# A gate applied to two projections apart, with the sum moved to GpSimd

## The reference

```
attn = windowed_attn(xn, W_qkv, W_O, b_O)      # 16 heads, windows of 64
ug = xn @ W_ug + b_ug
g = sigmoid(ug[..., S_DIM:])
states: s = A * s + (xn @ B_w + u)             # a scan over the tokens
y_ssm = states @ C_w
x = x + g * attn + (1.0 - g) * y_ssm
```

## Time and profile before

| what | value |
|---|---|
| median of 3 runs | 1922.1 us (1920.32 to 1922.23) |
| profiled execution, first to last instruction | 1963.7 us |
| mean granted TensorE clock | 0.973 of full speed |
| mixer stage | from 0 to about 818 us |
| one batch of the mixer | about 48 us |

### The profile page before, as it was taken

One profiled execution on the slowest core, in us unless ns is written; L12 is line 12 of the kernel. 1 busy time (PEld: TensorE's weight loads), 2 busy tenths in 40 slices (PEclk: granted clock), 3 DMA queues, 4 the chain that ended last, 5 costly groups with the idle time before them and its releaser, 6 DMA issues. The chain is left out here.

```text
span 1963.7 us, 66143 instructions
## 1 busy us (share of the span) xinstructions
PE 1768.1 (90%) x23600; PEld 1357.0 (69%) x23601; DVE 1414.5 (72%) x3235; ACT 1000.3 (51%) x1810; POOL 1074.9 (55%) x1304
## 2 busy tenths in 40 slices
PE   4999999999999999799888988809999999999997
PEld 2677776777777677466555655508888888888886
DVE  7788888888888887478778878744656656656665
ACT  3444444444444444455464555306665565565564
POOL 5333334444333332457777777754666666666664
PEclk8999999999999999899999999959999999999998
DMA  5322222222222222254344345313545545555553
GB/s 153 90 77 79 73 72 72 72 72 73 72 73 74 73 75 69 93 162 140 112 139 147 112 129 155 95 34 81 93 89 94 88 92 94 89 91 94 90 91 56
DMA packets 165756, 183.06 MB, mean 93 GB/s; under 512 B 37188, under 2 KB 146439, under 8 KB 165440
## 3 DMA queue, kind: packets, MB, share of 16 engines
q1 hardware_dynamic: 111360, 105.03, 19.2%
q0 software_dynamic: 36352, 56.78, 15.7%
q10 hardware_dynamic: 17856, 18.37, 2.7%
HBM read 109.14 MB, written 62.38 MB: 87 GB/s over the span
## 5 line engine op out<-in xcount | busy, mean ns | idle before, releaser
L1980 POOL DMA_INDIRECT out<-experts_y,experts_entry x144 | 237.2, 1647 | 192.6 <-DVE experts_y L1956 162.6
L1921 DVE TENSOR_SCALAR experts_v<-experts_v 128x512 f32<-128x512 f32 x144 | 73.8, 512 | 227.6 <-ACT experts_v L1895 213.7
L856 ACT ACTIVATE mixer_prob<-mixer_sc 128x1024 f32<-128x1024 f32 x128 | 131.2, 1025 | 165.9 <-PE mixer_sc L699 165.9
L1895 ACT ACTIVATE experts_g<-experts_pg,x_b 128x256 f32<-128x256 f32 x288 | 120.7, 470 | 184.1 <-PE experts_pv L132 184.0
L1970 POOL DMA_INDIRECT experts_rows<-scratch_xs,experts_entry x144 | 169.2, 1175 | 50.6 <-issue 50.3
L987 DVE TENSOR_REDUCE w_mx<-mixer_sc 128x8 bf16<-128x1024 f32 x128 | 156.3, 1221 | 22.7 <-PE mixer_sc L673 22.7
L130 PE MATMUL experts_pg<-experts_xT,x_w 128*128 128x256 f16 x576 | 158.2, 275 | 11.8 <-issue 8.0
L1603 POOL DMA_INDIRECT scratch_queue<-mlp_entry,mlp_slot x128 | 139.1, 1087 | 43.9 <-issue 39.3
L130 PE MATMUL experts_py<-x_w,experts_hh 128*128 x576 | 157.7, 274 | 2.0 <-DVE experts_hl L1933 2.0
L1116 POOL TENSOR_TENSOR mixer_oTl<-mixer_on,mixer_oTh 128x128 f16<-128x128 f32 x128 | 54.8, 433 | 190.4 <-ACT mixer_oTh L866 190.1
L132 PE MATMUL experts_py<-x_w,experts_hl 128*128 x576 | 157.8, 274 | 0.0
(11 more groups left out here) (378 smaller groups left out, 5699.0 us busy)
## 6 DMA issues: line engine op xcount, KB each, us to landing
w_Kz<-mixer_Kt SPq DMA_DIRECT2D x64, 128.0 KB, 2.7
mixer_hres<-mixer_h SPq DMA_DIRECT2D x16, 512.0 KB, 4.4
scratch_xs<-scratch_mod SPq DMA_DIRECT2D x64, 128.0 KB, 3.5
scratch_x<-w_x SPq DMA_DIRECT2D x16, 512.0 KB, 2.9
scratch_n<-w_x SPq DMA_DIRECT2D x32, 256.0 KB, 2.3
w_nrm<-scratch_n SPq DMA_DIRECT2D x16, 512.0 KB, 4.3
mlp_stage<-in_x_w SPq DMA_DIRECT2D x16, 512.0 KB, 4.1
mlp_xb<-scratch_x SPq DMA_DIRECT2D x16, 512.0 KB
```

The costliest lines, as they stand in the source:

```text
L856: act.activation(prob[:, n % 2, :].rearrange("p (c j) -> p c j", c=2), sc[:, 2:4, :], ACT.Exp, scale=SCALE).then_inc(exped.sem, 1)
L1895: act.activation(dst[:, q, f * ROWS:(f + 1) * ROWS], bank[:, q, f * ROWS:(f + 1) * ROWS], fn, bias=x["b1"][:, bass.ds(e, 1), bias + 2 * q ...
L1921: dve.tensor_scalar(v[:, q, :], v[:, q, :], -8.0, 10.0, ALU.max, ALU.min).then_inc(v_cut.sem, 1)
L1980: pool.indirect_dma_start(out=out, out_offset=bass.IndirectOffsetOnAxis(ap=entry[:, s, t, 0:1].bitcast(I32), axis=0), in_=y[:, s % 2, t, : ...
```

## The change

The state output is no longer subtracted on TensorE. The left half of the PSUM bank now holds attention alone, and `nc` and its three matmuls for each tile are gone. GpSimd turns tanh into the gate g = 0.5 tanh + 0.5, in two operations of 128x512 for each batch. VectorE makes share = attention x g and mix = (g - 1) x state output. GpSimd sums share + hres, and then subtracts mix: two operations for each tile where there was one.

```
-    def negate(self, dve):
-        dve.wait_ge(self.low.sem, 6)
-        for part in range(2):
-            dve.tensor_scalar(self.w["nc"][part][:], self.w["c"][part][:], -1.0, None, ALU.mult
-                              ).then_inc(self.shaped.sem, 1)
...
+        share = m.sb("share", [P, TT, D])
...
# TensorE, outputs(b, t)
-                hi_lo_products(pe, att, [sth[:, tok], stl[:, tok]], [a[:, 0, :] for a in w["nc"]], False, False)
...
# VectorE, mix_tokens(b, t)
                 if t == 0:
-                    dve.wait_ge(gate_sb.sem, gate_sb.at(b, 2))
+                    dve.wait_ge(opened.sem, opened.at(b, 2))
+                    dve.wait_ge(x1_part.sem, x1_part.at(b, 0))
                 dve.wait_ge(out_mm.sem, out_mm.at(b, t + 1))
-                dve.scalar_tensor_tensor(out=mix[:, t, :], in0=mix[:, t, :], scalar=1.0, in1=out_bank[t][:, 0:D],
-                                         op0=ALU.add, op1=ALU.mult).then_inc(gated.sem, 1)
+                dve.tensor_tensor(share[:, t, :], out_bank[t][:, 0:D], mix[:, t, :], ALU.mult).then_inc(gated.sem, 1)
                 dve.wait_ge(gated.sem, gated.at(b, t + 1))
-                dve.scalar_tensor_tensor(out=mix[:, t, :], in0=mix[:, t, :], scalar=0.5,
-                                         in1=out_bank[t][:, D:], op0=ALU.mult, op1=ALU.add
-                                         ).then_inc(mixed.sem, 1)
+                dve.scalar_tensor_tensor(out=mix[:, t, :], in0=mix[:, t, :], scalar=-1.0, in1=out_bank[t][:, D:],
+                                         op0=ALU.add, op1=ALU.mult).then_inc(mixed.sem, 1)
...
# GpSimd, body(b, last)
                 inverse_deviation(NB if last else b + 1, 1)
+                for u in range(2):
+                    wait_alone(pool, gate_sb.sem, gate_sb.at(b, u + 1), pool_passed)
+                    pool.tensor_scalar(mix[:, 2 * u:2 * u + 2, :], mix[:, 2 * u:2 * u + 2, :], 0.5, 0.5, ALU.mult,
+                                       ALU.add).then_inc(opened.sem, 1)
                 if last:
                     for j in range(6, 9):
                         start.low_part(pool, j, start.low)
...
                 for t in range(TT):
+                    pool.wait_ge(gated.sem, gated.at(b, t + 1))
+                    pool.tensor_tensor(x1[:, t, :], share[:, t, :], hres[:, t, :], ALU.add).then_inc(x1_part.sem, 1)
+                    pool.wait_ge(x1_part.sem, x1_part.at(b, t + 1))
                     pool.wait_ge(mixed.sem, mixed.at(b, t + 1))
-                    pool.tensor_tensor(x1[:, t, :], mix[:, t, :], hres[:, t, :], ALU.add).then_inc(x1_sb.sem, 1)
+                    pool.tensor_tensor(x1[:, t, :], x1[:, t, :], mix[:, t, :], ALU.subtract).then_inc(x1_sb.sem, 1)
```

More of the change, by code:

```diff
@@ L497, in mixer @@
         gate_sb = m.counter("gate_sb", 2)
+        opened = m.counter("opened", 2)
         gated = m.counter("gated", TT)
+        x1_part = m.counter("x1_part", TT)
         mixed = m.counter("mixed", TT)
@@ L776, in body @@
                     if s == NW:
-                        made_once(b, (start.shaped, 3))
+                        made_once(b, (start.shaped, 1))
                         outputs(b, 0)
@@ L980, in body @@
                         start.low_part(dve, j, start.low)
-                    start.negate(dve)
                 if not last:
@@ L2043, in program @@
                 halves("c", 1, D)
-                halves("nc", 1, D)
                 for name in ("bg3", "bo3"):
```

## The result

| | median | lowest to highest | runs |
|---|---|---|---|
| before | 1921.49 us | 1920.32 to 1922.23 | 4 |
| changed | 1934.3 us | 1931.66 to 1936.43 | 4 |

The ratio is 1.0069, with an interval of 1.0057 to 1.0081: the change costs 13.3 us by the ratio. The direction was as forecast and the time lies in the range; the loss is 2.2 times the +5.9 of the point.

A forecast was written before the change was run, and what follows sets the result against it. TensorE was taken to bound the mixer, with GpSimd time before the first oTl reaching it undiminished. The terms -16.5 + 20.7 + 1.7 = +5.9 us gave 1928.0 us, range 1920 to 1944.

The forecast's parts named there:

- Part 1: TensorE's outputs at the batch seam: dropping 192 products with nc returns 1.10 us a seam, -16.5 us.
- Part 2: GpSimd before the first oTl: two gate openings, 1.31 us a pair, reach TensorE undiminished, +20.7 us.
- Rivals one and three: Gate openings: one, the pair costs 2.3 us, 1944, chance 0.10; three, the pair costs nothing, 1907, chance 0.08.
- rival four: Near balance: the pair costs 1.2 us and the seam returns the full 1.31; +1.0, 1923 us, chance 0.20.
- Part 3: GpSimd's eight x1 sums delay SyncE's store, keys and hres copy; TensorE's 0.56 us idle covers the keys; priced at nothing.
- Rival two: Late modulate on GpSimd collides with VectorE's scan, costing 1.0 us in 14 batches; 1942 us, chance 0.20.
- Part 4: Mixer's end, behind the last batch: no seam hides the eight x1 sums, +1.7 us.

The follow-up runs named there:

- e2: Changed kernel with SyncE's store of x1 issued in the next batch, behind the keys and the copy to hres; 1922.74 us, ratio 1.0000.
- e5: Kernel before without the three products with nc and nothing in their place, so the state output is not subtracted; 1899.83 us, ratio 0.9894.
- e4: Kernel before with only the pair of gate openings added, writing a tile nobody reads, mix_tokens waiting for it; 1941.1 us, ratio 1.0087.
- e8: Changed kernel with the store of x1 moved behind the next batch's keys but ahead of the copy to hres; 1926.68 us, ratio 1.0018.
- e6: Kernel before with each x1 sum made twice, first into a tile nobody reads; 1926.28 us, ratio 1.0032.
- before again: Kernel before, unchanged, run and profiled a second time; 1919.6 us, ratio 0.9999, profiled span 1917.6 us.
- e1: Changed kernel with the two gate openings ahead of the second inverse deviation on GpSimd; 1918.78 us, ratio 0.9973.
- e9: Changed kernel with x1's store behind keys and hres copy, and openings plus last batch's low parts ahead of the second inverse deviation; 1901.72 us, 0.9886.
- e7: Changed kernel with the store of x1 issued by GpSimd right behind its sums, and SyncE's store gone; 1928.33 us, ratio 1.0030.

## Why the prediction was partly right

**Part 1, the products: right.** `outputs(0)` was to give 0.33 and gave 0.34 (C). The rest of the seam was to give 0.77: in e2 and e5, where the keys are on time, D fell by 0.80 and 0.84. In the changed kernel this was earned and taken back at the next step.

**Part 2, the pair: right, a little high.** An opening took 623 ns for my 0.67, and two take 1.21 for 1.31; an estimate from the earlier trace rows of an operation that the trace did not have was 7% off. The estimate by the Trainium skill, GPSIMD Engine Reference, sections 3.1 and 4.1, was 0.64, and the 623 ns agree with it. A grew by 1.20, so the wait passed through VectorE, the copy to `shift` and TensorE undiminished, as the last batch had shown. e4 gives the term alone as +16.7 instead of +20.7; 2.7 of the 4.0 are the 0.19 a batch in B, of which below. Rivals one and three are out. Of rival four, the pair's 1.2 us came true and the seam's full 1.31 did not (1.14).

**Part 3, the sums: this is the step that failed.** The text had the sums taking 6.57 us from the start of the first one, and they took 6.44 (326.46 to 332.90). It had the keys start 7.42 behind that point, and they started 7.51 behind. It had the last key land 12.6 behind (339.9 against 327.28), and TensorE went on 13.75 behind. I took the last key's flight as 2.7 us, the median of all 64 transfers of before; it took 4.1 (336.06 to 340.16). The four transfers now follow the 512 KB store by 0.9 us (333.07 to 333.97), where before it was 2.1. I had TensorE want the keys at 339.57 and covered the rest with 0.56, leaving 0.23 us to spare by a sum of five terms, and wrote "Price nothing". The true figure is 0.84 to 0.89 us a batch, 12.6 in 15. The text did give the price for the case that the cover is gone, a us for a us, but it gave that case no chance, and none of the rivals was it.

The margin was smaller than the spread that the trace of before showed: the keys' landing there has its median at 2.7 us and its maximum at 4.4. It is also a wrong reading of the batch shown. There the last key did not land near 338.9 but at 340.37, 4.1 us behind its issue, and the fourth transfer of a batch took 3.4 to 4.4 us in 8 of 15 batches of before (3.9 or more in 14 of 15 after the change). With 4.1 in place of 2.7 the prediction's own sum has the key land at 341.3 against 340.13, so 1.2 us a batch instead of nothing. The late flight was there before the change; the change took away the time that hid it.

That the time lies in the range owes something to luck. The upper part of the range stood there for rivals one and two, and neither of them is what filled it.

**Rival two: real, smaller, and hidden here.** `modulate` did start late and ahead of the scan (341.40 against 342.58), and the scan's median rose from 1993 to 2183 ns, its maximum to 2467, not over 3000. The keys had delayed the scan itself, and the two met less than in e8, where `modulate` starts some 0.7 us ahead of the scan and not 1.2: A of the changed kernel (18.71) is that of e2 (18.73), where the scan takes 1998. So it cost nothing in the changed kernel, and 0.28 a batch where it was provoked in e8.

**Part 4, the end: right in kind, a little small.** The extra sums were to cost 1.7, and with the last batch's 1.3 for the pair the stretch from the last scan to the MLP was to grow by 3.0. It grew by 3.4, and a further 0.9 followed. Alone, the parts give +2.9 (sums, e6), -0.9 (products, e5) and +2.0 (pair, e4) in this stretch. The rows, of the changed kernel and then of before again:

```profile
804.94 0.61 PE L684 MATMUL mixer_sc<-w_twoI,w_maskq 64*128 64x512 bf16 x2 [9.59 <-DVE w_shift L1005]
...
824.41 0.72 POOL L1123 TENSOR_TENSOR w_x<-w_x,mixer_mix 128x256 f32<-128x256 f32 x1
...
826.33 1.94 PE L1290 MATMUL mlp_pj<-w_identf,w_nrm 128*128 128x128 f32 x8 [5.80 <-PEq L405]
```

```profile
812.14 0.72 POOL L1122 TENSOR_TENSOR w_x<-mixer_mix,mixer_hres 128x256 f32<-128x256 f32 x1 [0.70 <-DVE mixer_mix L957]
...
814.05 1.10 PE L1289 MATMUL mlp_pj<-w_identf,w_nrm 128*128 128x128 f32 x8 [2.91 <-PEq L411]
```

TensorE now idles 5.80 us instead of 2.91 ahead of the MLP, and its first eight transposes then take 1.94 us instead of 1.10. That this is the 0.9 is not shown: in e4 and e5 the idle time is 2.91 and the transposes take 1.06, and yet the time from there to the end is 1105.3 and 1106.0 us, against 1103.6 in before again and 1104.4 in the changed kernel.

**What was not foreseen and went the other way.** B lost 0.19 us a batch. TensorE had paused without a releaser ("issue") for a moment before L721 in the profiles of before:

```profile
321.58 0.42 PE L721 MATMUL mixer_pv<-mixer_prob,w_halfone 128*32 128x128 f32 x5 [0.16 <-issue]
```

The two profiles of before differ in B as well (9.77 and 9.51), and B is 9.32 also in e4, which keeps the products. So it is not the products, and the cause stays open; with a kernel that differs from itself by 0.26, it may not be an effect of the change at all. It is worth 2.7 us of the account.

**The sum.** In the pieces of the account, forecast and measured against before again:

| piece | forecast | measured |
|---|---|---|
| up to the second scan: a seam and batch 0's pair | -1.10 + 1.10 = 0 | -1.05 |
| 14 periods | 14 x (1.31 - 1.10) = +2.9 | +9.9 |
| last scan to the MLP: the last pair and part 4 | 1.3 + 1.7 = +3.0 | +3.4 |
| behind it | 0 | +0.9 |
| sum | +5.9 | +13.2 |

The 7.0 us too few in the periods are the keys, +11.8 (0.84 x 14), less three things that went better than forecast: B, -2.7; the pair, -1.5 (0.11 x 14); the products, -0.6 (1.14 for 1.10). The first piece was not taken apart, and its -1.05 is within what two profiles of before differ by. Without the keys' 11.8 the change would stand at +1.4 us, and e2, which takes them away, measures 1.0000.

## What to carry to other kernels

Where work is moved onto an idle engine, its price is set by what is queued behind it and who waits for that, not by the engine's busy share: the same 1.2 us a batch cost 16.7 us (e4) behind the chain of small operations and nothing ahead of it (e1), where 8 us at once did cost (e9). Follow a longer stretch of work past the next queue too: a store that waits for it also holds every load that stands behind the store, and putting the store last was worth 13 us with no arithmetic changed. And where the slack left by a sum of several terms is smaller than the spread of a transfer's landing in the trace, price it with that spread, and read the landing of the very transfer that the argument is on, not the median of its group. Savings elsewhere (TensorE arriving earlier) use up the slack from the other side.

## What the runs showed of the hardware

A key transfer of 128 KB lands after 2.5 us at the median and 2.9 at the most where the store of x1 comes behind the keys (e2). With the 512 KB store 0.9 us ahead in the same queue the maximum is 5.3, with 2.1 us between them it was 4.4, and with the store on another engine's queue 5.2. It is mostly the fourth transfer of a batch that is slow. How the slower landing comes about between the two transfers was not measured; that it does not need SyncE's queue is what e7 shows.

A small VectorE operation can be held for microseconds while GpSimd runs a long one: 3.98 us for 0.17 in e9.

TensorE's granted clock around the MLP's first matmuls, in the columns of the earlier trace rows. The changed kernel first, whose MLP starts at 826.33:

```profile
826.00:828.00 2.00, 1.67 (x8) 1.57 (x8) 0.00 (x0) 0.55 (x1) 0.57 (x6) 0.50 0.74 262
...
834.00:836.00 2.00, 2.00 (x6) 0.76 (x5) 1.73 (x10) 0.51 (x1) 0.00 (x0) 0.50 1.09 385
836.00:838.00 2.00, 2.00 (x10) 0.86 (x9) 0.85 (x3) 1.45 (x3) 0.34 (x1) 0.91 0.94 341
```

Then before again, whose MLP starts at 814.05:

```profile
814.00:816.00 2.00, 1.10 (x8) 0.85 (x8) 0.00 (x0) 1.28 (x2) 0.46 (x6) 0.74 0.65 229
...
820.00:822.00 2.00, 2.00 (x7) 0.70 (x5) 1.66 (x11) 0.69 (x1) 0.00 (x0) 0.56 1.06 377
822.00:824.00 2.00, 2.00 (x11) 0.88 (x9) 1.83 (x7) 1.19 (x2) 0.01 (x1) 1.00 1.10 389
```

A share of 0.50 is the 1.2 GHz level. Both kernels fall to it, behind 5.80 us of idle time and behind 2.91. Behind the longer one the first eight transposes already run at the lower level (1.94 us for 1.10), and the full clock is back some 10 us behind the MLP's start and not 8.

The other place is the last batch, behind the long wait for the copy to `shift` (9.59 us after the change, 8.42 in before again), changed kernel and then before again, each from 0.1 us behind the end of the wait:

```profile
805.00:810.00 5.00, 5.00 (x101) 3.80 (x103) 2.50 (x5) 2.28 (x5) 0.85 (x2) 0.60 0.00 0
```

```profile
795.00:800.00 5.00, 5.00 (x121) 4.03 (x121) 3.02 (x5) 2.23 (x5) 0.85 (x2) 0.71 0.02 3
```

From the end of the wait to a scores-by-key matmul three steps on it takes 7.55 us (804.94 to 812.49) and took 7.04 (794.89 to 801.93): 0.5 us, which is about what the end lost beyond the forecast 3.0.

One profiled execution of an unchanged kernel can have a stage 40 us longer than another (500.3 against 460.2 in the MLP), while eleven timed runs of it lay between 1916.3 and 1924.7 us. A single profile should be read for differences inside a repeated piece, not for a stage's length.
